# Row scores in two pairs of PSUM banks with one maximum per pair, and no bank of their own for the side tasks

## The reference

```python
mod = (silu(c) @ wmod).reshape(8, 6, 1, -1)          # sa, ca, ga, sb, cb, gb
h = layernorm(x) * (1 + ca) + sa
qkv = h @ w_qkv                                      # 16 heads of 8 channels
attn = softmax(q @ k.T / sqrt(128)) @ v
x = x + ga * (attn @ w_out)
h = layernorm(x) * (1 + cb) + sb
scores = softmax(h @ w_router)                       # 8 experts, the best 2 kept
y = sum over experts of comb * (silu(h @ w_gate) * (h @ w_up)) @ w_down
x = x + gb * y
```

## Time and profile before

| what | us |
|---|---|
| median of three runs (653.71 to 657.55) | 655.14 |
| the profiled execution, device time | 654.47 |
| its span, from first to last instruction | 652.8 |
| from one batch's start to the next in the attention stage | 48.6 |
| attention stage of eight batches | about 50 to 437 |
| TensorE busy, of the span | 601.1 (92%) |
| VectorE busy | 548.4 (84%) |
| ScalarE busy | 440.2 (67%) |
| GpSimd busy | 267.9 (41%) |

### The profile page before, as it was taken

The page is one execution under the profiler, slowest core; times in us unless marked ns, Lnnn a source line. Parts: engine busy times, 40 slices in busy tenths (PEclk is TensorE's granted clock), DMA queues, the critical chain, the costliest instruction groups (busy, mean ns, idle before and its releaser), DMA issues.

```text
span 652.8 us, 10459 instructions
## 1 busy us (share of the span) xinstructions
PE 601.1 (92%) x3349; PEld 277.6 (43%) x3349; DVE 548.4 (84%) x1039; ACT 440.2 (67%) x837; POOL 267.9 (41%) x384
## 2 busy tenths in 40 slices
PE   4299999999999999999999999897999999999995
PEld 3112222332322322322322322236777777777773
DVE  3698889999999999999999999528788888888884
ACT  1207878879788788888878878774655555555552
POOL 4431112222222222222222212436576776776763
PEclk9757999999999999999999999999899999999998
DMA  7712703403404303404304401173244445444401
GB/s 190 174 64 52 223 4 87 144 19 84 148 20 97 135 20 92 141 20 98 133 21 99 133 20 47 47 204 104 98 131 153 132 135 154 134 132 152 136 19 33
DMA packets 49094, 65.77 MB, mean 101 GB/s; under 512 B 9544, under 2 KB 30544, under 8 KB 49040
## 3 DMA queue, kind: packets, MB, share of 16 engines
q1 hardware_dynamic: 46416, 64.32, 34.1%
q10 hardware_dynamic: 2624, 0.79, 0.5%
HBM read 47.26 MB, written 17.83 MB: 100 GB/s over the span
## 4 chain that ended last, share of the span: by engine, by line
PE 47%; DVE 20%; POOL 15%; ACT 8%; issue 7%; DMA 1%; SPq 1%; POOLq 0%; DVEq 0%; ACTq 0%
PE o_acc L1198 16%; PE s_row L1171 14%; POOL hid_lo L601 11%; DVE negmax L850 8%; DVE probs L1060 7%; PE s_col L1184 7%; ACT probs L645 3%; ACT hid_hi L786 3%; POOL h_lo L607 2%; PE misc L1136 1%; PE misc L1152 1%; PE misc L1122 1%; PE misc L1119 1%; DVE probs L1050 1%; SPq L306 1%
## 5 line engine op out<-in xcount | busy, mean ns | idle before, releaser
L850 DVE TENSOR_REDUCE negmax<-s_row 128x1 f32<-128x512 f32 x512 | 321.7, 682 | 32.1 <-PE s_row L1171 30.7
L645 ACT ACTIVATE probs<-s_col 128x512 f32<-128x512 f32 x512 | 273.3, 598 | 67.1 <-PE s_col L1184 64.1
L1171 PE MATMUL s_row<-k_stack,q_stack 64*128 64x512 bf16 x512 | 140.8, 402 | 23.2 <-DMA k_stack<-k_scr 10.9
L601 POOL TENSOR_TENSOR hid_lo<-probs,hid_hi 128x512 fp32r<-128x512 f32 x87 | 128.8, 1497 | 62.5 <-ACT hid_hi L786 62.5
L1198 PE MATMUL o_acc<-probs,v_aug 128*32 128x512 f32 x1024 | 136.4, 605 | 0.0
L1184 PE MATMUL s_col<-q_stack,k_stack 64*128 64x512 bf16 x512 | 127.4, 380 | 3.3 <-ACT probs L645 2.7
L786 ACT ACTIVATE hid_hi<-probs 128x512 fp32r<-128x512 f32 x88 | 55.7, 633 | 85.7 <-DVE probs L1060 85.7
L1171 PEld LDWEIGHTS s_row<-k_stack,q_stack 64*128 64x128 bf16 x512 | 35.4, 93 | 176.9 <-DVE negmax L850 133.7
L1060 DVE TENSOR_TENSOR probs<-probs,q_stack 128x512 f32<-128x512 f32 x56 | 61.9, 1106 | 15.4 <-POOL hid_lo L601 14.3
L509 POOL CAST negmax_parts<-negmax 128x16 bf16<-128x16 f32 x32 | 6.3, 198 | 166.1 <-DVE negmax L850 166.1
L1050 DVE TENSOR_TENSOR probs<-probs,s_col 128x512 f32<-128x512 f32 x88 | 59.5, 677 | 2.9 <-ACT probs L806 1.6
(11 more groups left out here) (138 smaller groups left out, 684.0 us busy)
## 6 DMA issues: line engine op xcount, KB each, us to landing
q_scr<-q_parts SPq DMA_DIRECT2D x48, 128.0 KB, 2.4
k_scr<-k_parts SPq DMA_DIRECT2D x48, 128.0 KB, 2.4
q_stack<-q_scr SPq DMA_DIRECT2D x8, 768.0 KB, 6.5
k_stack<-k_scr SPq DMA_DIRECT2D x8, 768.0 KB, 7.8
q_stack<-combT_scr SPq DMA_DIRECT2D x24, 256.0 KB, 3.4
k_stack<-combT_scr SPq DMA_DIRECT2D x16, 224.0 KB, 3.0
q_stack<-combT_scr SPq DMA_DIRECT2D x16, 192.0 KB, 2.8
q_stack<-combT_scr SPq DMA_DIRECT2D x16, 160.0 KB, 2.5
```

What stands on the lines that cost most here:

```text
L601: nc.gpsimd.tensor_tensor(hid_lo[k % HIDDEN][:], weighed[(par + k) % 2], hid_hi[k % HIDDEN][:], ALU.subtract).then_inc(s["hid_split"], 1)
L645: nc.scalar.activation(probs[t % 2][:, j, :], s_col[score_bank("col", u)][:], ACT.Exp, scale=INV_SCALE).then_inc(s["exp_done"], 1)
L850: nc.vector.tensor_reduce(negmax[n % 2][:, j, qc:qc + 1], s_row[score_bank("row", u)][:], AX.X, ALU.max, negate=True).then_inc(s["row_max" ...
L1171: nc.tensor.matmul(s_row[score_bank("row", u)][:], q_stack[par][at:at + KS, head // 2, P * qc:P * (qc + 1)], k_stack[par][at:at + KS, head ...
```

## The change

- Row scores: the three banks become two pairs, `s_row[0]` and `s_row[1]`, each of 2 x 512. TensorE writes the row scores of two heads into a pair, one after the other, and signals once; VectorE takes both maxima with one instruction over 128 x 2 x 512. A slot becomes: row pair, col 0, col 1, [step 0], row pair, col 2, col 3, [step 1], weigh, [step 2].
- `misc` is gone. Side tasks that VectorE empties (`BY_VECTOR`: o0, o1, proj, router) take a place in the round of the row pairs; all others take a place in the round of the three column banks, now `ring`. Two lists, `ROWS` and `COLS`, give every score and task its place. A place in the rows waits for the reader of the place two before, a place in the ring for the reader three before, whatever it held. The shift of `score_bank` goes.
- Parts of q and k of batches 1 to 7: ScalarE copies the whole product into `q_rest`, `k_rest`; GpSimd then makes the high part, the rest, the middle and the low part (four instructions where it had one). VectorE's subtraction and ScalarE's middle part go. Batch 0 stays as it was.
- xT of a batch is transposed a batch earlier, at (14, 0) instead of (0, 0), and `normalise1` on GpSimd goes with it.
- In the expert stage the gate and up products take the two pairs, and the last transposes take `ring`.

```diff
+    BY_VECTOR = ("o0", "o1", "proj", "router")
+    ROWS = [(0, t, half) for t in range(AHEAD) for half in range(2)]
+    COLS = [None] * (RING - 1) + [("max0", 0)]
+    for b in range(B):
+        for t in range(SLOTS):
+            of, at = (b, t + AHEAD) if t + AHEAD < SLOTS else (b + 1, t + AHEAD - SLOTS)
+            for step in range(3):
+                if step < 2:
+                    if of < B:
+                        ROWS.append((of, at, step))
+                    COLS += [(b, t, 2 * step), (b, t, 2 * step + 1)]
+                if (t, step) in schedule(b):
+                    task = schedule(b)[t, step]
+                    (ROWS if task[0] in BY_VECTOR else COLS).append(task)
...
-                nc.vector.tensor_reduce(negmax[n % 2][:, j, qc:qc + 1], s_row[score_bank("row", u)][:], AX.X, ALU.max,
+                nc.vector.tensor_reduce(negmax[n % 2][:, 2 * half:2 * half + 2, qc], s_row[ROW_PLACE[b, t, half] % 2][:], AX.X, ALU.max,
                                         negate=True).then_inc(s["row_max"], 1)
...
+            def row_free(place):
+
+                if place >= 2:
+                    what = ROWS[place - 2]
+                    if len(what) == 2:
+                        free(what[1], what[0])
+                    else:
+                        b, t, half = what
+                        pe.wait_ge(s["row_max"], ROW_PAIRS * b + 2 * t + half + 1)
+
+            def col_free(place):
+
+                what = COLS[place - RING]
+                if what and len(what) == 2:
+                    free(what[1], what[0])
+                elif what:
+                    b, t, j = what
+                    pe.wait_ge(s["exp_done"], UNITS * b + G * t + j + 1)
...
+            def split(b, n, rest, high, middle, low):
+
+                pool.wait_ge(s[f"{n}_rest_ready"], b + 1)
+                pool.wait_ge(s[f"{n}_stored"], 16 * STORES * b)
+                pool.sem_inc(s["waited"])
+                nc.gpsimd.tensor_copy(high, rest[:]).then_inc(s[f"{n}_high"], 1)
+                pool.wait_ge(s[f"{n}_high"], b + 1)
+                nc.gpsimd.tensor_tensor(rest[:], rest[:], high, ALU.subtract).then_inc(s[f"{n}_step"], 1)
+                pool.wait_ge(s[f"{n}_step"], b)
+                pool.sem_inc(s["waited"])
+                nc.gpsimd.tensor_copy(middle, rest[:]).then_inc(s[f"{n}_mid"], 1)
+                low_part(b, low, rest, middle, f"{n}_mid", f"{n}_split")
```

More of the change, by code:

```diff
@@ L568, in body @@
             def body(b, par, first, last):
-                if not last:
-                    normalise1(b + 1)
+                if first:
+                    normalise1(1)
                 split_max(b, 1)
@@ L769, in body @@
                         if at == ROUTER_EXP and not first:
-                            evacuate(None, b - 1, 1 - par, "router")
-                        name = TASKS.get(at)
-                        if name in tasks(first, last) and name != "router" and not (last and name in ("x1T", "combT")):
-                            of = owner(b, name)
-                            evacuate(misc_use(b, first, last, name), of, 1 - par if of is not b else par, name)
+                            evacuate(None, b - 1, 1 - par, "router", None)
+                        name, of = schedule(b).get(at, (None, None))
+                        if name not in (None, "router") and not (last and name in ("x1T", "combT")):
+                            evacuate(misc_use(b, at), of, of % 2, name, task_bank(name, of))
             over_batches(act, body)
@@ L1147, in task @@
                     for k in range(CH):
[L1148 removed]
+                        last = nc.tensor.transpose(ps[:, P * k:P * (k + 1)], x1n[:, k, :], ident[:])
                 elif name == "router":
@@ L1166, in row_scores @@
                     pe.wait_ge(s["stacked_first"], 16 * LOADS * (b + 1))
-                if t == CH and j == 0:
+                if t == CH and half == 0:
                     pe.wait_ge(s["stacked"], 16 * LOADS * (b + 1))
-                if not (isinstance(b, int) and b == 0 and u < SCORES):
-                    pe.wait_ge(s["row_max"], UNITS * b + u + 1 - score_distance("row", u))
-                nc.tensor.matmul(s_row[score_bank("row", u)][:], q_stack[par][at:at + KS, head // 2, P * qc:P * (qc + 1)],
-                                 k_stack[par][at:at + KS, head // 2, :], start=True, stop=True).then_inc(s["row_ready"], 1)
+                row_free(place)
@@ L1174, in col_scores @@
+                for i in range(2):
+                    head = G * n + 2 * half + i
+                    at = 64 * (head % 2)
+                    last = nc.tensor.matmul(s_row[place % 2][:, i, :], q_stack[par][at:at + KS, head // 2, P * qc:P * (qc + 1)],
+                                            k_stack[par][at:at + KS, head // 2, :], start=True, stop=True)
+                last.then_inc(s["row_ready"], 1)
             def col_scores(b, par, t, j):
@@ L1181, in col_scores @@
                     pe.wait_ge(s["max_loaded"], 32 * (group(b, n) + 1))
-                if not (isinstance(b, int) and b == 0 and u < SCORES):
-                    pe.wait_ge(s["exp_done"], UNITS * b + u + 1 - score_distance("col", u))
-                nc.tensor.matmul(s_col[score_bank("col", u)][:], k_stack[par][at:at + KS, head // 2, P * kc:P * (kc + 1)],
+                col_free(place)
+                nc.tensor.matmul(ring[place % RING][:], k_stack[par][at:at + KS, head // 2, P * kc:P * (kc + 1)],
                                  q_stack[par][at:at + KS, head // 2, :], start=True, stop=True).then_inc(s["col_ready"], 1)
@@ L1208, in _ @@
             for j in range(NJ):
-                last = nc.tensor.matmul(s_col[1][:, B * j:B * (j + 1)], wmod_sb[:, C * j:C * (j + 1)], cT[:], start=True, stop=True)
+                last = nc.tensor.matmul(ring[1][:, B * j:B * (j + 1)], wmod_sb[:, C * j:C * (j + 1)], cT[:], start=True, stop=True)
             last.then_inc(s["mod_full"], 1)
@@ L1280, in _ @@
             pe.wait_ge(s["w_split"], 3)
-            pe.wait_ge(s["row_max"], UNITS * B)
+            pe.wait_ge(s["row_max"], ROW_PAIRS * B)
+            free(B - 2, "proj")
+            free(B - 2, "router")
             def product(out_ps, w_hi, w_lo, k, hi, lo, start, stop):
```

277 lines of the change are left out of this document (127 added, 150 removed).

## The result

| | before | changed |
|---|---|---|
| median of 18 runs each, us | 654.66 (651.50 to 657.55) | 658.73 (657.49 to 661.32) |
| profiled execution, us | 654.47 | 658.46 |
| its span, us | 652.8 | 656.6 |

The ratio is 1.0063 (95%: 1.0054 to 1.0073): the change makes the kernel slower by 0.63%. Forecast was 657.5, or +0.4%.

What follows compares the result with a forecast made beforehand. Loops between engines, not one engine, bound the kernel. Batches 1 to 6 +3.9, batch 0 -0.4, batch 7 +0.3 and prologue -1.2 make +2.6 on 654.47: 657.1, or 657.5 for a median; range 645 to 665.

Steps and rivals of the forecast that it cites:

- the waits at the shared banks: Slots with side tasks: a ring task at step 0 makes 3.10 us, a row task at step 0 makes 3.24.
- slot 7: Batches 1 to 6: VectorE's relief covers the wait for its layer-norm statistics; 2.61 us (-0.41).
- batch 7: No q, k, v: slot 1 gains some 0.7, o1, attnT and combT pay 0.3 to 0.5 each; net +0.3.
- expert stage: Same work in other banks, so 0.
- The two loops: Slots without a side task: VectorE's loop of 2.71 us binds before the change, ScalarE's loop is 2.61.
- Slot 5: Slot with attnT and max2: 3.10 us plus 0.20 for max2.
- Prologue: VectorE's 32 maxima back to back become 16 pairs at 1.12 us: -1.2.
- GpSimd's slack: `split_max` of group 2 ends at 14.0 us, TensorE wants max2 at 15.7: slack 1.7, cost 0.
- the rival on it: GpSimd comes too late for max2, with all scores behind it: 660 at casts of 1.16, 666 at 1.4; 11%.
- the rival of 1.36: VectorE's maximum of a pair costs two singles, 1.36 us: kernel 668, halfway 663; 12%.
- advice on large tiles: Rival that VectorE's relief goes through in full, 3.8 us in each of six batches: 634; 6%.
- The ring wait doesn't bind: Exponentials start earlier, task slots run at TensorE's pace, slots 10, 14 and 15 stay at 2.70: 644; 17%.

Runs made afterwards that it cites:

- The first experiments on tasks and on the pair: Changed kernel with all side tasks in the ring, 656.11 us; changed kernel with each pair's maxima taken by two instructions of 512, 662.04 us.
- the kernel with two maxima a pair: Changed kernel, each row pair reduced by two instructions of 512 elements instead of one of 1024: 662.04 us, ratio 1.0128.
- GpSimd's share alone: Kernel before, only with the parts of q and k of batches 1 to 7 made on GpSimd from one ScalarE copy: 654.18 us, ratio 0.9989.
- the kernel with three more GpSimd instructions: Changed kernel plus three unread GpSimd subtractions of 128 x 512 per batch, between the splits of q and k: 671.50 us, ratio 1.0265.
- the orders tried here: `weigh` ahead of column score 3: changed kernel 668.54 us, with all tasks in ring 677.30, kernel before 685.55; `weigh` halved: changed 655.32, before 662.73.

## Why the prediction was right, and where its sizes were off

The forecast of +0.4% is +0.63% by the measurement, with the sign as argued and, for the losses, the mechanism too: the waits at the shared banks. For the gains the mechanism was right in the plain slots and in part wrong in slot 7, as told below. Two of its sums are slightly off: 657.1 and 0.7 are 657.8 and not 657.5, and 32 x 0.08 is 2.6 and not 2.4; neither changes the forecast's sense. Measured, the wide instruction spares VectorE 14.2 us in 256 pairs (540.7 against 526.5), 1.8 a batch. Against the profiled executions (+4.0 on 654.47, where +2.6 was forecast), from the starts of `weigh` in both traces:

| stretch | forecast | measured |
|---|---|---|
| to the first `weigh` (58.10, then 57.98) | -1.2 | -0.1 |
| batch 0 | -0.4 | -0.2 |
| batches 1 to 6 | +3.9 | +4.1 |
| batch 7, to its last `weigh` (436.97, then 441.98) | +0.3 | +1.2 |
| expert stage | 0 | -1.2 |
| span | +2.6 | +3.8 |

- **The two loops.** Right: slots without a task at 2.60 to 2.61, ring tasks at 3.09 to 3.10, row tasks at 3.25, and the waits at the scores named. The first experiments on tasks and on the pair moved just the slots that these loops own.
- **Slot 7** came out as forecast (2.60 for 2.61), but not by the relief that the forecast names. VectorE's work is not shorter in the kernel with two maxima a pair, and slot 7 is 2.61 there; it is 3.02 with GpSimd's share alone. The round of the pairs does it.
- **Slot 5** was mis-sized by 0.15, from six batches 0.9 us. The term left out is a DMA issue on ScalarE. Timeline of the changed kernel, slot 5:

```profile
213.40 0.27 ACT L718 ACTIVATE negmax_T<-ring 48x128 bf16<-48x128 bf16 x1
213.52 0.38 PE L1216 MATMUL ring<-q_stack,k_stack 64*128 64x512 bf16 x2
213.70 0.33 ACTq L680 DMA_DIRECT2D max_scr<-negmax_T  x1
...
214.13 1.09 ACT L668 ACTIVATE probs<-ring 128x512 f32<-128x512 f32 x2 [0.46 <-PE ring L1216]
```

  ScalarE copies the transposed maxima (to 213.67), then issues their store, which waits for that copy and takes 0.33, and only then comes to the first exponential, 0.61 behind column score 0 instead of 0.41. The sum closes: 1.00 from `weigh` to max2's transpose, 0.27 to the copy, 0.27 of it, 0.03, 0.33 of the issue, 0.10, 1.09 of two exponentials, 0.04 to column score 3 and 0.32 to `weigh` are 3.45.
- **Other slots.** Slots 8 and 12 came out 0.05 and 0.09 shorter. Twice a slot was longer by 0.28, once each (slot 9 of batch 1, slot 1 of batch 6). Batch 6 has no xT to make, which the forecast's six equal batches overlook: its slot 14 is 2.60. These nearly cancel against slot 5, which is luck.
- **Prologue.** The pairs follow each other every 1.13 as forecast, but the first row score came 0.52 later (32.40, before 31.88): the loads ahead of it landed later (x 2.95 instead of 2.76, the k stack 4.38 instead of 4.08), which the change doesn't touch. From there to the first column score the gain is 0.95 of the 1.2 (19.18 to 18.23). Between the first column score and the first `weigh` 0.3 more is lost (7.04 to 7.35), and that is TensorE's clock: the scores just ahead of the first `weigh` take 0.61 and 0.64 where they took 0.40 and 0.38, at a granted clock between 57 and 59 us of 0.67 against 0.85. In the kernel with three more GpSimd instructions, whose prologue is the same, the clock was back earlier (q's products last 1.12, not 2.07) and the first `weigh` starts at 55.87, so single executions differ here by more than the term itself.
- **Batch 7** is the term that was worst: I counted o1, attnT and combT, and left out x1T in slot 10 (+0.49) and o0. Slot 1 gained its 0.70.
- **Expert stage.** 0 was right for the change as far as the traces show; the 1.2 us go with the clock (last section), and without them these two executions would be 5.0 apart. That they make the sum look better is luck.
- **GpSimd's slack** of 1.7 was measured as 1.5 with the three added instructions; the rival on it had no wait at max2 to show.
- **The pair's price**, 1.22 us, ended the rival of 1.36. The estimate of 1.19 from the formula of the Trainium skill ("VectorE: DVE Perf Modes", the TRN2 errata) is 0.03 under the trace's 1.220, so the two agree within 3%. What its advice on large tiles would have promised the kernel, 634 us, did not come, since at most 3.3 us hang on the wide instruction (the two-instruction kernel).
- **The ring wait doesn't bind**, the rival at 644, is out: the waits at column score 3 are in the trace, and a fourth bank in the ring takes them away.

What the study adds is where the gain went. The pairs take VectorE's loop out of the plain slots and slot 7, but they use four of the eight banks, and the side tasks lose their own. The kernel with a ring of four gives the pairs up, keeps the rest of the change and is ahead of both. Which part of its 9.3 us on the changed kernel the fourth bank gives and which the third row bank, no run separates.

## What to carry to other kernels

Write down each loop between engines as a sum of rows (start to start, through the bank's reader and back), and the slot length follows to some hundredths; an engine's relief is worth only the distance to the next loop, here 0.09 us of 2.70. A deeper round can relieve an engine's loop where less work on it would not. Count DMA issues too: here one stands for 0.33 us ahead of ScalarE's exponential. When a round of n buffers serves more than n uses per pass, some use closes a chain through everything issued since its reader was released, the long group too. In the orders tried here moving that group did not open the chain; a further buffer did. Before merging buffers to save instructions, count what the lost buffer was holding apart.

## What the runs showed of the hardware

- *Two different clocks after the same idle.* In the kernel before, TensorE's granted clock fell to half speed (1.2 GHz) in the expert stage after an idle of 1.96 us, and came back some 3 us later; in the changed kernel it stayed at 2.4 GHz after an idle of 1.97 us at the same place. Timelines of TensorE at the transposes of x1n and the expert matmuls behind them, before:

```profile
456.93 1.05 PE L1148 MATMUL misc<-ident,x1n 128*128 128x128 f32 x4 [1.96 <-DVE x1n L1043]
457.63 0.78 PE L1285 MATMUL s_row<-h_hi,wg_hi 128*128 128x512 f32 x1
...
461.06 0.95 PE L1152 MATMUL misc<-wr_sb,h2T 128*128 128x8 f32 x8
```

  and changed:

```profile
461.95 0.63 PE L1161 MATMUL ring<-ident,x1n 128*128 128x128 f32 x4 [1.97 <-DVE x1n L1056]
462.34 0.48 PE L1307 MATMUL s_row<-h_hi,wg_hi 128*128 128x512 f32 x1
...
464.51 1.06 PE L1165 MATMUL ring<-wr_sb,h2T 128*128 128x8 f32 x8
```

  The granted clock of the kernel before between 458 and 460 us (busy us and count of each engine, then the clock):

```profile
458.00:460.00 2.00, 2.00 (x6) 1.52 (x6) 1.39 (x3) 1.87 (x4) 1.16 (x1) 0.50 0.22 45
```

  From the transposes to the router it took 4.13 us at the lower clock and 2.56 at full, 1.57 apart; the span's lead in this stage came to 1.2. Of the fourteen profiled executions nine show the slow form (3.89 to 4.13 us) and five the full clock (2.56), in kernels of either layout, so it does not go with the banks. Whether it goes with the kernel or with the execution one profile of each can't tell, and what decides it no run shows.
- *A half-width matmul costs more than half.* Eight passes of 256 columns take 0.57 us to the next row score, eight of 512 take 1.00.
- *A DMA issue that waits for ScalarE's own result delays its next instruction.* In slot 5 above the store of the maxima is issued from 213.70 for 0.33 us, and the exponential whose score was started at 213.52 starts at 214.13. The kernel before has the same in its slot 5: issue from 212.50 for 0.33, score at 212.32, exponential at 212.92.
- *GpSimd's cast* of 128 x 512 from float32 to bfloat16 takes 0.61 us, half its subtraction of the same tile (1.15).
